# One run of pieces for eight shared experts, and a third place in the ring of the second alignment

## What is computed

```
x = x + align(context, layernorm(x))       # per batch: 64 x 1601 distances, dynamic time warping, backtrack,
                                           # then each token adds the context rows that its path passes
x = x + recurrence(layernorm(x))           # 16 heads, gated linear recurrence over 64 steps, RMS norm, output matrix
h = layernorm(x)
x = x + sum of 2 of 8 experts(h) + shared expert(h)     # hidden 704, silu(h w1) * (h w3) w2
```

## Time and profile before

| | |
|---|---|
| median of 3 runs | 1186.69 us |
| lowest and highest | 1186.13 and 1194.79 us |
| profiled execution, its own time | 1189.48 us |
| span of the profiled execution | 1188.2 us |
| TensorE busy | 1010.7 us, 85% |
| VectorE busy | 663.2 us, 56% |
| ScalarE busy | 489.3 us, 41% |
| mean granted TensorE clock | 0.939 of full speed |

### The profile page before, as it was taken

One profiled execution on the slowest core, in us unless ns is written; L12 is line 12 of the kernel. 1 busy time (PEld: TensorE's weight loads), 2 busy tenths in 40 slices (PEclk: granted clock), 3 DMA queues, 4 the chain that ended last, 5 costly groups with the idle time before them and its releaser, 6 DMA issues.

```text
span 1188.2 us, 15519 instructions
## 1 busy us (share of the span) xinstructions
PE 1010.7 (85%) x4892; PEld 597.8 (50%) x4892; DVE 663.2 (56%) x2316; ACT 489.3 (41%) x839; POOL 115.9 (10%) x150
## 2 busy tenths in 40 slices
PE   5886639888981899988897599888999999999998
PEld 2332213333330455544665365646676767676776
DVE  4994859999999667587569613436411111111116
ACT  4884726666770445323331154232222222222221
POOL 1000000000000000000000000000243434252210
PEclk9998979999996899989898799788899999999999
DMA  9999954565777889240050097394122222123015
GB/s 353 323 304 272 267 154 144 159 192 155 229 217 204 275 276 341 89 160 0 1 184 1 0 340 239 99 354 167 48 73 62 77 65 78 60 78 110 31 48 183
DMA packets 123806, 190.47 MB, mean 160 GB/s; under 512 B 9008, under 2 KB 93136, under 8 KB 123728
## 3 DMA queue, kind: packets, MB, share of 16 engines
q1 hardware_dynamic: 117840, 171.13, 46.4%
q0 software_dynamic: 5888, 18.36, 5.1%
HBM read 165.43 MB, written 24.03 MB: 159 GB/s over the span
## 4 chain that ended last, share of the span: by engine, by line
PE 56%; DVE 30%; DMA 5%; issue 4%; ACT 3%; SPq 2%; POOL 0%; DVEq 0%; ACTq 0%; POOLq 0%
PE bank L1791 13%; PE bank L1638 8%; PE bank L1822 7%; PE bank L1659 4%; DVE table L807 4%; PE bank L1783 4%; DMA spaced<-dist 3%; DVE beyond L823 3%; DVE passed L828 3%; PE bank L1802 3%; PE bank L1814 2%; DVE col_min L800 2%; PE bank L1565 2%; DVE z L744 2%; DVE stays L777 2%
## 5 line engine op out<-in xcount | busy, mean ns | idle before, releaser
L1009 DVE TENSOR_TENSOR hid<-bank,act_s 128x352 f32<-128x352 f32 x104 | 54.2, 523 | 230.5 <-PE bank L1791 178.8
L1791 PE MATMUL bank<-w_up,srcT 128*128 x512 | 162.9, 460 | 0.7 <-ACT srcT L1411 0.7
L1549 PE MATMUL bank<-sq,ones 128*64 128x402 f32 (+1 forms) x512 | 101.0, 515 | 37.9 <-ACT sq L1274 37.8
L1419 ACT ACTIVATE act_s<-bank 128x352 f32<-128x352 f32 x104 | 48.0, 464 | 202.0 <-PE bank L1791 120.7
L1791 PEld LDWEIGHTS bank<-w_up,srcT 128*128 128x128 f32 x512 | 96.0, 189 | 47.9 <-issue 4.1
L1565 PE MATMUL bank<-table,ident 128*128 128x402 f32 x144 | 67.9, 555 | 57.7 <-DVE stays L777 48.5
L1543 PE MATMUL bank<-ctxT,latT 128*64 128x402 f32 (+1 forms) x512 | 102.1, 520 | 5.4 <-DMA ctxT<-ctx_tr_dram 4.7
L1274 ACT ACTIVATE sq<-ctxT 128x1608 f32<-128x1608 f32 x64 | 97.5, 1526 | 10.4 <-DMA ctxT<-ctx_tr_dram 10.4
L1638 PE MATMUL bank<-rows_c,on_path 128*64 128x256 f32 (+1 forms) x832 | 100.7, 394 | 0.8 <-ACT on_path L1336 0.5
L1822 PE MATMUL bank<-w_dn,hidT 128*128 (+1 forms) x384 | 93.6, 380 | 0.4 <-DVE y_sb L1023 0.4
L1311 ACT ACTIVATE code<-bank,unpassed 128x402 bf16<-128x402 f32 x72 | 42.2, 590 | 120.5 <-PE bank L1567 120.5
(11 more groups left out here) (291 smaller groups left out, 1630.3 us busy)
## 6 DMA issues: line engine op xcount, KB each, us to landing
rows_c<-ctx_nat_dram SPq DMA_DIRECT2D x32, 896.0 KB
ctxT<-ctx_tr_dram SPq DMA_DIRECT2D x32, 804.0 KB, 8.3
ctxT<-ctx_tr_dram SPq DMA_DIRECT2D x32, 797.0 KB, 7.9
rows_c<-ctx_nat_dram SPq DMA_DIRECT2D x32, 640.0 KB
spaced<-dist SPq DMA_DIRECT2D x128, 101.0 KB, 4.0
w_up<-w_t_dram SPq DMA_DIRECT2D x16, 704.0 KB, 13.0
table<-spaced SPq DMA_DIRECT2D x48, 202.0 KB, 4.5
w_dn<-w_t_dram SPq DMA_DIRECT2D x16, 256.0 KB, 5.4
```

The costliest lines, as they stand in the source:

```text
L1009: e.tensor_tensor(hid[i][:, :], psum[2 * i + 1][:, 0:HH], act_s[i][:, :], ALU.mult).then_inc(hid_done, 1)
L1549: last = e.matmul(ps[b * T:(b + 1) * T, 0:nq], ones[:, 0:T], sq[i][:, b, k, 0:nq], start=False, stop=(k == KC - 1))
L1791: last = e.matmul(psum[2 * i + m][:, 0:HH], srcT[t % 2][:, k, :], w_up[:, bass.ds(ex, 1), m, k, columns], start=(k == 0), stop=(k == KC - 1))
```

## The change

`MINIMA = [2, 3]` makes the rings of `col_min` and `stays` three places deep for the second alignment alone. The third place lies in the area of the first context buffer, which is free by then; two waits and a memset of its edge column guard and clear it. All that went by `q % 2` and `q - 2` goes by `minima_slot` and `q - MINIMA[g]`, on VectorE and TensorE. `experts(RUNS[0])` and `experts(RUNS[1])` become one run of eight units (18 pieces in place of 10 + 10), of which eight pieces go beside `recurrence(1)`: `shared_beside` gives pieces up to its n = 23 alone. On VectorE a `pause()` stands ahead of them.

```diff
+MINIMA = [2, 3]
...
+def minima_slot(g, q):
+    return q % MINIMA[g]
...
 def shared_beside(n):
-    return 1 if n >= 14 and n % 5 != 4 else 0
+    return 1 if 14 <= n < 24 and n % 5 != 4 else 0
...
+        contexts_at = cursor[0]
+        col_min.append(place("col_min2", [CB, L]))
+        stays.append(place("stays2", [CB, LW], BF16))
+        assert cursor[0] <= align_end
+        at(contexts_at)
...
             def code_stays(g, q):
-                tb, k0, n, i = table[g], q * CB, code_width(q), q % 2
-                if q >= 2:
-                    e.wait_ge(coded, g * CODES + q - 1)
+                tb, k0, n, i, places_ = table[g], q * CB, code_width(q), minima_slot(g, q), MINIMA[g]
+                if q >= places_:
+                    e.wait_ge(coded, g * CODES + q - places_ + 1)
...
             def code_final(g, q):
-                k0, n, i = q * CB, code_width(q), q % 2
+                k0, n, i = q * CB, code_width(q), minima_slot(g, q)
...
             def align(g):
-                tb = table[g]
+                tb, places_ = table[g], MINIMA[g]
+                if g:
+                    e.wait_ge(product, UNITS)
+                    e.wait_ge(squared, UNITS)
+                    e.memset(stays[2][:, :, L:LW], 0.0).then_inc(third_clear, 1)
+                    e.wait_ge(third_clear, 1)
                 e.wait_ge(table_in, TABLE_IN[g])
...
-                    low = col_min[q % 2][:, at, :]
+                    low = col_min[minima_slot(g, q)][:, at, :]
...
-                    if at == 0 and q >= 2:
-                        e.wait_ge(gapped, half_count(g, q - 2, 1))
+                    if at == 0 and q >= places_:
+                        e.wait_ge(gapped, half_count(g, q - places_, 1))
...
-                    if at == 1 and q >= 2:
-                        code_final(g, q - 2)
+                    if at == 1 and q >= places_:
+                        code_final(g, q - places_)
...
-                for q in range(CODES - 2, CODES):
+                for q in range(CODES - places_, CODES):
                     code_final(g, q)
...
             interleave(align(1), chain(add_rows(range(0, 4)), pause(), together(recurrence(0), add_rows(range(4, 8))),
-                                       beside(recurrence(1), experts(RUNS[0]), shared_beside), experts(RUNS[1])),
+                                       beside(recurrence(1), chain(pause(), experts(RUNS[0] + RUNS[1])), shared_beside)),
                        behind_second)
...
             def code_gap(g, q, h):
-                i, steps = q % 2, half_steps(q, h)
+                i, steps = minima_slot(g, q), half_steps(q, h)
```

More of the change, by code:

```diff
@@ L487, in build @@
         dist_out = [sem(f"dist_out{i}") for i in range(DISTS)]
-        filled, padded, table_in = sem("filled"), sem("padded"), sem("table_in")
+        filled, padded, table_in, third_clear = sem("filled"), sem("padded"), sem("table_in"), sem("third_clear")
         step_done, stayed, gapped, barred, edged, coded, back_done, termed, spread = (
@@ L1510, in scalar_program @@
             interleave(align(1), chain(add_rows(range(0, 4)), together(recurrence(0), add_rows(range(4, 8))),
-                                       beside(recurrence(1), experts(RUNS[0]), shared_beside), experts(RUNS[1])),
+                                       beside(recurrence(1), experts(RUNS[0] + RUNS[1]), shared_beside)),
                        behind_second)
```

## The result

| | before | after |
|---|---|---|
| median of the timed runs, us | 1187.49 (1182.92 to 1194.79, 16 runs) | 1180.14 (1177.37 to 1185.25, 16 runs) |
| ratio, 95% interval | | 0.9938 [0.9925, 0.995] |
| profiled execution, span | 1188.2 | 1179.7 (takes 1180.9) |

The change saves 0.62% (7.35 us by the medians; 5.9 to 8.9 by the interval): within the 1% that was called no change, yet clear of noise, as the interval leaves out 1. The forecast was 1180.8 us, worked out from a median before of 1186.69 us (3 runs).

A forecast was written before the change was run, and what follows sets the result against it. VectorE was taken to end the stage from 380 us to `path_terms`, with TensorE's list fixed behind it. Terms -2.6 - 3.0 + 0.1 - 0.4 = -5.9 us took 1186.69 to 1180.8 us; range 1179.3 to 1183.5, wider 1176 to 1188.

The forecast's parts named there:

- the narrow range: The forecast's own range for the time, 1179.3 to 1183.5 us, given a chance of 0.52.
- Part 1, the ring while TensorE sets the pace: Second alignment, up to about 504 us: third place ends TensorE's stalls before gaps; 2.6 us gained, bounds 0 and 2.6.
- Part 2, first half: 504 to 543 us: VectorE's first wait for a gap, 1.69 us, ends; 0.3 is lost again, 1.4 us gained.
- Part 2, second half: 504 to 543 us: VectorE's second wait for a gap, 1.61 us, ends; 1.6 us gained.
- Part 3: Ring's added memset and waits at the stage's start cost 0.1 us; the third `code_final` hides in a wait.
- Part 4, the one run: Gate of `recurrence(1)`: R24 goes before gate_hidden(7), VectorE then waits for the exponential; 0.4 us gained, bounds -1.3 and +5.
- the clock comes up: Rival: shorter pauses keep TensorE at 2.4 GHz in 515 to 545 and 571 to 580 us; 1176.8 us, chance 0.12.
- TensorE's list after it is fixed: Behind VectorE's end of the stage at `path_terms`, everything moves by the same amount as VectorE gains.
- slower: Rival: TensorE stays at the low level for experts pieces 9 to 17 and VectorE waits; 1184 or 1199 us, chance 0.08.
- the waits come back elsewhere: Rival: loads of rows and evictions hold TensorE, so part 1 gives nothing, part 2 only 1.6; 1184.8 us, chance 0.2.

The follow-up runs named there:

- Run 3: Changed kernel with SyncE issuing the first chunk's store of `latents` ahead of two loads of rows: 1178.27 us, ratio 0.9935 to the kernel before.
- both edits: Changed kernel with the store of `latents` issued earlier and the gate's exponential moved ahead of a piece of experts on ScalarE: 1177.85 us, ratio 0.9912.
- run 2: Kernel before with only the one run of pieces and VectorE's pause, both alignments keeping two places: 1186.28 us, ratio 0.9987.
- the exponential's kernel: Changed kernel with seven ScalarE pieces beside the recurrence, not eight, so the gate's exponential comes earlier: 1179.37 us (0.9931), again 1177.91 us (0.9907).
- The halves alone: Kernel before with only the third place, 1183.91 us (0.9974), and with only the one run and pause, 1186.28 us (0.9987).
- runs 10 and 11: Eight memsets delaying VectorE before `path_terms`, in the changed kernel with the exponential earlier (1180.98 us) and in the changed kernel itself (1182.70 us).

## Why the prediction was right, and where it wasn't

The time, 1180.14 against 1180.8 us, is right. The sum of -5.9 us is the small end of what was measured (-5.9 to -8.9), and the stage, on which it was made, lost 6.5. But it is right in part by luck, by terms that cancel: in the stage 1.6 us were booked that didn't come, and some 2.9 us of its first half came that weren't booked (1.8 of TensorE's busy time, 1.1 in the first 9 us); behind the stage more was gained that nobody forecast; and the forecast started from a median 0.8 us below the one that the result is measured against. The lower end of the narrow range is off by a slip: with the bounds of parts 2 and 4 (-0.3 and -0.9) it is 1179.6, not 1179.3.

**Part 1, the ring while TensorE sets the pace: as forecast.** 2.6 us expected. 1.42 + 0.58 + 0.58 = 2.6 went, less 0.17 of a wait for rows. That the stall belonged to VectorE's `stays`, not to the eviction that the row names, is borne out by what remained: the eviction's own 0.84.

**Part 2, first half: as forecast.** 1.4 us expected, 1.38 measured (1.96 to 0.58), with the 0.3 lost again as a wait of 0.29.

**Part 2, second half: the step that failed.** "Both end with a ring of three" was true of the wait for the gap, but the 1.6 us booked for the second were not gained. From the first gate to the next projections it is 24.2 to 24.4 us in the four traces without the third place and 23.8 to 24.9 us, 24.2 in the mean, in the eight with it and the store in its old place. Two things were wrong. The size was that of one trace: the wait is 1.61 and 1.43 us in two of the four traces, 0.40 in the two others, and the stretch is as long in all. And I had named what is late next for the first wait and not for the second. It was the store of `latents`, issued behind loads of rows: 1.28 us, and 0.30 to 1.58 in the eight traces. Run 3 shows that this wait goes when the store is issued earlier. What goes with it isn't settled: 1.6 to 2.3 us in that trace, 0.2 to 0.3 with both edits, where TensorE comes back at the lower level. That level has its share in the kernel after too: gap products of 1.68 and 1.55 us, behind which the transposes start at 540.49, 0.9 us after VectorE's `hn` was ready. A queue that the moved step doesn't stand in can hold it all the same.

**Part 3: as forecast.** The memset takes 0.06 us, and from the start of `path_terms` to the first `col_min` it is 1.28 us in place of 1.14: 0.14 against 0.1, ahead of the stage. The final step of the ring hid in waits for ScalarE, which are now 0.87 and 0.97 us.

**Part 4, the one run: as forecast.** -0.4 expected; -0.4 between the second RMS norm and `path_terms`, and -0.2 to -0.4 for the stage in run 2. The exponential came as worked out: VectorE goes on 8.41 us after the gate's product starts (613.91 - 605.50), where 8.55 (615.9 - 607.35) was expected. The table load took 1.28 us with nothing before it. The rule of the Trainium skill, "ScalarE: Activation LUTs", section "What ACT_TABLE_LOAD costs", with a switch at about 2.66 us, is not what this kernel shows, before or after.

**The rival "the clock comes up" was partly right, in other places.** With the third place the clock of the first half is 1.00 in place of 0.98, 1.8 us in busy time, in nine of ten traces, and in none of the four without. In the first 9 us of the stage another 1.1 us came. That piece takes 8.6 to 9.1 us in the four traces without the third place and 7.6 to 8.7 us in the ten with it, so it is partly chance, and partly perhaps the ring. Of the places that were named, 515 to 545 us stayed at 0.83, and the 9 us from the second RMS norm on stayed low too (0.53 before from 571 us, 0.52 after from 569 us).

**What nobody forecast: the rest.** "TensorE's list after it is fixed", so the rest would move rigidly. The list is fixed, the clock isn't. All five traces of kernels with the one run, the pause and the old place of the exponential have a rest of 508.4 to 509.3 us; the nine others have 511.9 to 516.7. The timed runs bear that out in part only: one run alone should be 5 us faster by its trace and is 1.5 (-0.4 to 3.3); the kernel after, 8.5 and 11.5 us faster by its two spans against the first of the kernel before, is 7.35. The traced executions aren't the middle ones either: the five with a short rest took 0.9 us less in the mean than the median of their kernel, the nine others 1.2 us more, so about 2 of the 5 us may be the choice of execution. But without the pause, with the same stage, the time is 4.5 us longer, and a stage 3.6 to 5.4 us shorter buys the exponential's kernel 0.8 to 2.5. So I hold that part of the gain of 7.35 us is the rest's clock, 1 to 4 us by an estimate from these differences; no run shows it by itself. The halves alone add up to 4.6 us of the 7.35, but their intervals are too wide to show that the two together do more.

**What stays open** is why the clock of the rest goes with the order of work ahead of it. It isn't the moment counted from the start of the span (runs 10 and 11), nor the length of TensorE's idle time before `path_terms` (8.35 to 11.0 us in the five traces with a short rest, 8.3 to 13.8 in the others), nor how long the other engines are busy in it. The Trainium skill, "TensorE: Matmul & The Clock Gate", section "HAM oscillation — how this bites in real kernels", describes pauses that leave the array slow afterwards. The loss at 769.89 us is of that kind, and it goes with a longer pause: 1.8 to 2.1 us where it happens, 0.7 to 1.2 where it doesn't. The pause in turn goes with the level of the products ahead of it. Why that level comes back sooner in some kernels than in others no run shows.

**The rival "slower" didn't happen.** The piece after the long idle starts at the low level (0.90 us for three transposes at 624.01) and is at the higher one from 630.50 (0.49 us). TensorE is full up to 656 us, but VectorE never waits for it, and at 657.98 TensorE waits again. **The rival "the waits come back elsewhere"** happened at one place, the store, and hardly in the loads (0.17 us).

## What to carry to other kernels

For each wait that an edit takes away, look up every other semaphore on which the instructions behind it wait, the landing of stores among them, and when their release was issued: what is late next can sit in a queue that the edit never touches. When a row names a releaser that had finished long before, look for the second wait. A wait read from one trace can be chance: here 1.61 us in one trace and 0.40 in two others of the same kernel, so a second trace before the forecast would have shown how little the term was worth. And when TensorE paces what follows, compare its busy time for the same products in both traces before a gain is put down to the edited place: here some 5 us of span changed about 100 us behind it, with no instruction changed.

## What the runs showed of the hardware

- TensorE's granted clock in a stretch of unchanged work differed between kernels that were edited well ahead of it, and was alike in the two or three traces of one kernel: from `path_terms` to the first routed expert 170.0 to 170.9 us in five traces (149.4 to 150.1 of TensorE's busy time) and 173.5 to 178.3 (151.9 to 157.7) in the nine others.
- In this stretch a faster TensorE ended later: 16 products in 6.4 to 6.8 us, an idle time of 1.8 to 2.1 us, then projections that start at the lower level (nine traces); the same products in 7.4 to 7.9 us, 0.7 to 1.2 us idle, then projections at the higher level (five traces).
- After the same idle time of 4.3 us TensorE's next two gap products took 1.68 us in three traces, and 0.91, 1.06 and 1.29 us in three others.
- A store of `latents` took 10.1 to 10.6 us from its issue to the release of the waiting engine, in eight traces, and the profile calls this wait "issue".
- A table load took 1.28 us, with 0.02 us between it and the eviction ahead of it on ScalarE, and 0.01 us between it and the exponential.
